# A weight cast copied ahead of time in DRAM, its loads on another queue, and an ACT step reordered, in an eight-core scan and feed-forward kernel

## The chip, the cores and the metric

The kernel runs on the 8 cores of one Trainium2 chip. Each core does the same program on its own quarter of the work: one of 4 batches, one half of the 2048 positions (1024 columns, and 64 columns of history ahead of them). The cores don't talk to each other. The metric is the device time in microseconds (us) of the slowest core. The kernel before takes 2141.85 us (median of 3 runs, 2139.96 to 2142.64).

A core has these engines: TensorE (PE, matrix products), VectorE (DVE), ScalarE (ACT), GpSimd (POOL) and SyncE (SP). DMAs are issued here by POOL and by SP. Whatever POOL issues goes to a queue that the profile calls q0, software_dynamic; whatever SP issues goes to q1, hardware_dynamic. Both are served by the same 16 DMA engines of the core. In this kernel only POOL issues DMAs that change the type of the numbers on the way (float32 or int8 in memory, bfloat16 in the on-chip buffer).

## The reference, cut to what matters

```
x = x + layernorm(attn(layernorm(x)))        # layer "attn", a linear scan over positions
x = x + layernorm(ffn(layernorm(x)))         # int8 weights, silu(gate) * up, down

attn(x):  x_proj = x @ proj_in_w.T + proj_in_b
          delta  = softplus(x_proj @ B_w.T)
          h      = h * sigmoid(A) + x_proj_t * delta_t          (scan)
          y      = h.sum(states) @ C_w.T + D_param * x_proj
          return  (y @ proj_out_w.T + proj_out_b) + x
ffn(x):   down( silu((x @ w_gate) * s_gate) * ((x @ w_up) * s_up) ) * s_down
```

The sizes are 2048 channels, 8192 inner channels and 16 states. The change bears on `y @ proj_out_w.T` and on how its weight gets to the core.

## The kernel before, in words

Channels lie on the 128 partitions, in 16 tiles; the columns are positions. X, the input, stays in float32 in the on-chip memory (tile XT), loaded as three windows of columns: the last 64 columns by POOL, columns 0 to 511 (window 0 below) and 512 to 1023 (window 1) by SP. Every engine has one list of instructions, written in the order of the program and run in that order. `W(engine, tracker, value)` puts a wait on a counter into a list, `P` puts an instruction that counts up, `CB` makes an engine wait for its own last instruction, `DMA(queue, tracker, ...)` puts a transfer into a list, and `BAR` makes PE, DVE and ACT wait for each other. Nothing reorders the lists.

The stages, with their places in the profile of the kernel before:

- Constants. SP issues 13 small loads (L397), all counted on one tracker, and behind them the two large windows of X (L407). POOL issues its window of X, the small weight BWTT, and the first two of 16 tiles of the input weight (WRIT, L412).
- Pack (to 52 us). ACT waits for all 13 constants (the wait ahead of L421), then DVE and ACT build powers of sigmoid(A) in turns (L448, L461 on DVE, L457 on ACT).
- First layer norm (to 141 us). For each window, ACT makes a bfloat16 copy and a square of 16 tiles of XT (L485, L487), PE sums them over partitions, a short chain makes mean and scale, and DVE applies them (L573, L576), which writes XN1T. The order is: the 64 columns, window 0, window 1.
- Input projection (to 261 us): 16 output tiles, each with one weight tile WRIT of 128 x 2048, in two slots. POOL loads tile t+2 when PE is through tile t (L618).
- The scan, as products with packed powers (to 338 us), then `C_w` and `D_param` (to 393 us), which write YPRE: DVE writes the last of it at L739.
- Output projection (388 to 530 us), the stage that the change edits. 16 output tiles t; each has a weight tile WROT of 128 x 2048 in one of two slots and is done in two halves of 512 columns. POOL loads tiles 0 and 1 at L754 when PE is through the stage before, and tile t+2 at L822 when PE is through tile t. A half is 16 matmuls on PE; then ACT takes the sum out of PSUM and adds the bias (L779, into SQTT), DVE adds XN1T (L785), ACT squares the result (L792) and copies the half's columns of XT to bfloat16 (L797, into XBT, one buffer), and DVE multiplies that copy with the result (L803, into XYT). PE sums the three rows (result, square, product) over the partitions in `pend_sum`, which stands in PE's list behind the 16 matmuls of the next half; only after the last half does PE come to it at once. The tracker value that both the square's sum and DVE's product wait for is that of the second of the two ACT instructions, which is L797.
- Second layer norm (to 657 us), where the result is added to XT, and the feed-forward layer for the two windows in turn (to 2121 us), then the last store, issued by SP at L981.

Of the kernel before, what the change touches and what calls it, by code (L numbers as in the profile page):

```python
# [8 lines left out]
BF16 = mybir.dt.bfloat16  # L9
# [6 lines left out]
DT = 16  # L16
S = 16
TOUT = 1024
PAD = 64
# [49 lines left out]
def build_program(taps=()):  # L69
    nc = bass.Bass("TRN2", target_bir_lowering=False)  # L70

    d_x = nc.dram_tensor("xT", [128, DT * T], F32, kind="ExternalInput").ap()
    d_win = nc.dram_tensor("w_in_t", [DT, 128, 2048], F32, kind="ExternalInput").ap()
    d_wout = nc.dram_tensor("w_out_t", [DT, 128, 2048], F32, kind="ExternalInput").ap()
    d_bwt = nc.dram_tensor("b_w_t", [128, 256], F32, kind="ExternalInput").ap()
    d_cwt = nc.dram_tensor("c_w_t", [16, 2048], F32, kind="ExternalInput").ap()
    d_a = nc.dram_tensor("a_t", [128, 256], F32, kind="ExternalInput").ap()
# [17 lines left out]
    for tname, tshape, tdt in taps:  # L95
        tap_out[tname] = nc.dram_tensor("tap_" + tname, tshape, tdt,
                                        kind="ExternalOutput").ap()

    al = Alloc(SBUF_BYTES)
# [48 lines left out]
    o_xyt = al.pin(180224, 512 * 2, 4, 6, "xyt0")  # L148
    o_xyt2 = al.pin(209344, 512 * 2, 4, 6, "xyt1")
    o_xbt = al.pin(191232, 512 * 2, 4, 6, "xbt")  # L150
    o_invb0 = al.pin(206848, 512 * 2, 5, 7, "invb0")
    import os as _os
    if _os.environ.get("KDEBUG_ALLOC"):
# [6 lines left out]
    def Praw(eng, fn):  # L160
        plan[eng].append(fn)

    t_pe, t_vec, t_scl = Trk("t_pe"), Trk("t_vec"), Trk("t_scl")
# [4 lines left out]
    s_wro = [Trk(f"s_wro{i}", 16) for i in range(2)]  # L168
    s_wrf = [Trk(f"s_wrf{i}", 16) for i in range(4)]
    s_wrd = [Trk(f"s_wrd{i}", 16) for i in range(2)]  # L170
    s_out, s_tap = Trk("s_out", 16), Trk("s_tap", 16)
    DMAT = ([s_const] + s_x + [s_bwt, s_cwt] + s_wri + s_wro + s_wrf + s_wrd
            + [s_out, s_tap])
    TRKS = [t_pe, t_vec, t_scl] + DMAT
    ETRK = {"tensor": t_pe, "vector": t_vec, "scalar": t_scl}

    def DMA(queue, trk, build):
        trk.n += trk.step
        plan[queue].append(lambda e, b=build, t=trk: b(e).then_inc(t.h, t.step))
        return (trk, trk.n)  # L180

    def W(eng, trk, val=None):
        if val is None:
            trk, val = trk
        if val and val > 0:
            Praw(eng, lambda e, t=trk, v=val: e.wait_ge(t.h, v))

    def P(eng, fn):
        trk = ETRK[eng]
        trk.n += trk.step  # L190
        plan[eng].append(lambda e, b=fn, t=trk: b(e).then_inc(t.h, t.step))
        return trk.n
# [10 lines left out]
    def CB(eng):  # L203
        trk = ETRK[eng]
        Praw(eng, lambda e, t=trk, v=trk.n: e.wait_ge(t.h, v))
# [53 lines left out]
    def REG(name, off, part, cols, dtype):  # L259
        return nc.alloc_sbuf_tensor_at(name, [part, cols], dtype,  # L260
                                       offset=arena_base + off).ap()
# [29 lines left out]
    XYR0 = REG("XYR0", o_xyt, 1, 512, BF16)  # L291
    XYR1 = REG("XYR1", o_xyt2, 1, 512, BF16)
    XBT = REG("XBT", o_xbt, 128, 512, BF16)
    INVB0 = REG("INVB0", o_invb0, 128, 512, BF16)

    def SQT(i):
# [17 lines left out]
    def WRI(i):  # L314
        return WRIT[:, i * 2048:(i + 1) * 2048]
# [32 lines left out]
    def Xj(j, c0, c1):  # L348
        return XT[:, j * T + c0:j * T + c1]
# [7 lines left out]
    def YATT(j, l0, l1):  # L357
        return XPBT[:, j * T + l0:j * T + l1]
# [51 lines left out]
    for t in range(2):  # L410
        v_win[t] = DMA("gpsimd", s_wri[t % 2],
                       lambda e, t=t: e.dma_start(out=WRI(t % 2), in_=d_win[t]))  # L412

    P("vector", lambda e: e.memset(DLY, 0.0))
    v_dly = M("vector")
# [10 lines left out]
                                              in0=SCR[:, 0:256], scalar1=1.0))  # L426
# [6 lines left out]
                                       in1=SCR[:, 0:256]))  # L433
    CB("vector")
    P("vector", lambda e: e.tensor_mul(out=SIG8, in0=SCR[:, 256:512],
                                       in1=SCR[:, 256:512]))
# [10 lines left out]
    for o in range(1, NO):  # L447
        P("vector", lambda e, o=o: e.tensor_tensor(  # L448
            out=pkf4[:, :, o, :], in0=pkf4[:, :, o - 1, :], in1=siga3,
# [119 lines left out]
    def ln1_apply(wi, c0, c1, v_chain):  # L569
        wl = c1 - c0  # L570
        W("vector", t_scl, v_chain)
        for j in range(DT):
# [15 lines left out]
                                        in_=SRA1[0:1, PAD:PAD + 1024]))  # L588
    P("vector", lambda e: e.tensor_copy(out=XROWB[0:1, 0:1024],
                                        in_=SRB1[0:1, PAD:PAD + 1024]))  # L590
# [4 lines left out]
    for t in range(DT):  # L595
# [19 lines left out]
        if t + 2 < DT:  # L615
            W("gpsimd", t_pe, t_pe.n)
            v_win[t + 2] = DMA("gpsimd", s_wri[t % 2],
                               lambda e, t=t: e.dma_start(out=WRI(t % 2),  # L618
                                                          in_=d_win[t + 2]))
# [6 lines left out]
    for wi, (w0, w1) in enumerate(WIN3):  # L626
# [3 lines left out]
        for j in range(DT):  # L630
# [5 lines left out]
            out=SCR[0:16, 0:wl], in_=pb[b][0:16, 0:wl], func=AF.Exp))  # L636
        CB("scalar")
        P("scalar", lambda e, wl=wl: e.activation(
            out=SCR[0:16, 512:512 + wl], in_=SCR[0:16, 0:wl], func=AF.Ln,
# [3 lines left out]
            out=DB[:, w0:w1], in_=SCR[0:16, 512:512 + wl]))  # L643
# [6 lines left out]
    for wi, (w0, w1) in enumerate(WIN3):  # L650
# [7 lines left out]
            out=DR[:, w0:w1], in_=pb[b][:, 0:wl]))  # L658
# [8 lines left out]
    for k in range(2):  # L667
# [4 lines left out]
        for g in range(NG):  # L672
            for pi, (p0, p1) in enumerate(pieces):
# [3 lines left out]
                for j in range(DT):  # L677
# [6 lines left out]
                      out=GH(g, p0 - gb, p1 - gb), in0=pb[b][:, 0:pl],  # L684
                      in1=DR[:, p0:p1], op=ALU.mult))
# [3 lines left out]
            if g == 0:  # L689
                P("vector", lambda e: e.tensor_copy(  # L690
                    out=ACC1[:, 0:519], in_=GH(0, 57, 576)))
            else:
                c0 = 57 - 8 * g
                P("vector", lambda e, c0=c0, g=g: e.tensor_add(
                    out=ACC1[:, 0:519], in0=ACC1[:, 0:519],
                    in1=GH(g, c0, c0 + 519)))
# [10 lines left out]
        for o in range(NO):  # L707
# [5 lines left out]
            out=SHB[:, 512 * k:512 * (k + 1)], in_=pb[b][0:16, 0:512]))  # L713
# [10 lines left out]
    for t in range(DT):  # L724
        for wi in range(2):
            l0 = wi * 512
# [7 lines left out]
                out=SCR[:, 0:512], in_=XPBj(t, PAD + l0, PAD + l0 + 512),  # L734
# [5 lines left out]
                out=YPRE(t, l0, l0 + 512), in0=pb[b][:, 0:512],  # L740
                in1=SCR[:, 0:512]))
# [6 lines left out]
    BAR()  # L748
    WL2 = [(0, 512), (512, 1024)]
    v_wout = {}  # L750
    W("gpsimd", t_pe, t_pe.n)
    for t in range(2):
        v_wout[t] = DMA("gpsimd", s_wro[t % 2],
                        lambda e, t=t: e.dma_start(out=WRO(t % 2),  # L754
                                                   in_=d_wout[t]))
    W("tensor", t_vec, v_ypre)
    for b_ in (4, 5, 6, 7):
        pe_acquire(banks[b_])
    v_yatt_prev = {0: 0, 1: 0}
    sq_prev = {0: 0, 1: 0}  # L760
    xy_prev = {0: 0}
    xym_prev = {0: 0, 1: 0}
    pend_sum = None
    for t in range(DT):
        W("tensor", v_wout[t])
        for wi in range(2):
            l0 = wi * 512
            bk = banks[(t * 2 + wi) % 4]
            pe_acquire(bk)
            for j in range(DT):  # L770
                mm(pb[bk.idx][:, 0:512], WRO(t % 2)[:, j * 128:(j + 1) * 128],
                   YPRE(j, l0, l0 + 512), j == 0, j == DT - 1)
            bk.w_pe = t_pe.n
            if pend_sum is not None:
                pend_sum()
            sl = (t * 2 + wi) % 2
            W("scalar", t_pe, bk.w_pe)
            W("scalar", t_vec, v_yatt_prev[sl])
            P("scalar", lambda e, t=t, b=bk.idx, sl=sl: e.activation(  # L779
                out=SQT(sl)[:, 0:512], in_=pb[b][:, 0:512], func=AF.Identity,  # L780
                bias=BOUTC[:, t:t + 1]))
            vsc = M("scalar")
            bk.r_trk = (t_scl, vsc)
            W("vector", t_scl, vsc)
            P("vector", lambda e, t=t, l0=l0, sl=sl: e.tensor_add(  # L785
                out=YATT(t, l0, l0 + 512), in0=SQT(sl)[:, 0:512],
                in1=XN1j(t, PAD + l0, PAD + l0 + 512)))
            vv = M("vector")
            v_yatt_prev[sl] = vv
            W("scalar", t_vec, vv)  # L790
            W("scalar", t_pe, sq_prev[sl])
            P("scalar", lambda e, t=t, l0=l0, sl=sl: e.activation(  # L792
                out=SQT(2 + sl)[:, 0:512], in_=YATT(t, l0, l0 + 512),
                func=AF.Square))
            CB("scalar")
            W("scalar", t_vec, xy_prev[0])
            P("scalar", lambda e, t=t, l0=l0: e.copy(  # L797
                out=XBT, in_=Xj(t, PAD + l0, PAD + l0 + 512)))
            vsq = M("scalar")
            xyt_t = XYT0 if sl == 0 else XYT1  # L800
            W("vector", t_scl, vsq)
            W("vector", t_pe, xym_prev[sl])
            P("vector", lambda e, t=t, l0=l0, d=xyt_t: e.tensor_mul(  # L803
                out=d, in0=XBT, in1=YATT(t, l0, l0 + 512)))
            vxy = M("vector")
            xy_prev[0] = vxy

            def pend_sum(t=t, wi=wi, l0=l0, sl=sl, vv=vv, vsq=vsq, vxy=vxy,
                         xyt_t=xyt_t):
                W("tensor", t_vec, vv)  # L810
                mm(pb[6 if wi == 0 else 7][0:1, 0:512], ONESB,
                   YATT(t, l0, l0 + 512), t == 0, t == DT - 1)
                W("tensor", t_scl, vsq)
                sq_prev[sl] = mm(pb[4 if wi == 0 else 5][0:1, 0:512], ONESB,
                                 SQT(2 + sl)[:, 0:512], t == 0, t == DT - 1)
                W("tensor", t_vec, vxy)
                xym_prev[sl] = mm(pb[6 if wi == 0 else 7][32:33, 0:512],
                                  ONESB, xyt_t, t == 0, t == DT - 1)
        if t + 2 < DT:
            W("gpsimd", t_pe, t_pe.n)  # L820
            v_wout[t + 2] = DMA("gpsimd", s_wro[t % 2],
                                lambda e, t=t: e.dma_start(out=WRO(t % 2),  # L822
                                                           in_=d_wout[t + 2]))
    pend_sum()
    for b_ in (4, 5, 6, 7):
        banks[b_].w_pe = t_pe.n
# [173 lines left out]
    for k in range(2):  # L1000
        l0 = 512 * k
# [276 lines left out]
```

## Time and profile before

| | us |
|---|---|
| median of 3 runs | 2141.85 |
| the profiled execution's own time | 2140.66 |
| its span, first to last instruction, core 2 | 2139.0 |
| PE busy | 1754.3 (82%) |
| DVE busy | 415.2 (19%) |
| ACT busy | 335.1 (16%) |
| POOL busy | 155.3 (7%) |

The profile is of one execution on the slowest core. Its page gives for each engine the busy time and for 40 equal slices of the span the busy share in tenths; the granted PE clock and the share of the 16 DMA engines that is in use stand beside them. Two layers are to be told apart: the feed-forward layer fills the span from 657 us on, mostly with matmuls that follow each other closely, and the first 141 us hold only short sums. All eight cores have spans from 2134.7 to 2139.0 us.

### The profile page before, as it was taken

The numbers are of one execution on the slowest core, as the hardware profiler recorded it, in microseconds if no ns is written. First come the engines' busy times: TensorE is split into PE (matmuls) and PEld (weight loads), VectorE is DVE, ScalarE is ACT, GpSimd is POOL, SyncE is SP. The second block draws the span as 40 slices with busy tenths as digits, with TensorE's granted clock in tenths as the row PEclk, the third lists the DMA queues.
The fourth block names the chain that finished last, engine by engine and source line by source line (L and its number), as shares of the span: only waits on it lengthen the run. The fifth ranks groups of instructions, "written<-read, shape, count | busy, mean of one in ns | idle before, by whom it ended". The sixth has DMA issues, their size and how long they took to land.

```text
span 2139.0 us, 20851 instructions; the slowest of 8 cores (2134.7 to 2139.0 us)
## 1 busy us (share of the span) xinstructions
PE 1754.3 (82%) x8040; PEld 750.2 (35%) x8199; DVE 415.2 (19%) x705; ACT 335.1 (16%) x563; POOL 155.3 (7%) x295
## 2 busy tenths in 40 slices
PE   0659985698026999999999999799999999899980
PEld 0024441233013444444443333244444444333330
DVE  3440023222773111011100000311111011500005
ACT  3712202444010100110100000001101112000010
POOL 0000000000000000000001111000000000111100
PEclk9989997799568999999999999799999999999995
DMA  6014200233002443444333333234433443533322
GB/s 194 1 20 69 50 1 2 50 64 64 21 28 91 157 154 143 156 157 169 146 133 133 138 128 135 78 144 156 157 147 149 157 153 123 187 133 133 133 103 79
DMA packets 51509, 237.24 MB, mean 111 GB/s; under 512 B 5811, under 2 KB 6196, under 8 KB 35028
## 3 DMA queue, kind: packets, MB, share of 16 engines
q0 software_dynamic: 41792, 218.78, 30.8%
q1 hardware_dynamic: 9620, 17.11, 2.4%
q8 instruction: 68, 1.11, 0.2%
q14 instruction: 29, 0.24, 0.0%
HBM read 143.73 MB, written 8.39 MB: 71 GB/s over the span
## 4 chain that ended last, share of the span: by engine, by line
PE 71%; DVE 11%; DMA 9%; issue 3%; ACT 3%; DVEq 0%; SPq 0%; ACTq 0%; POOLq 0%
PE pb L225 71%; DMA WRDAT<-wd_t 4%; DMA WRDBT<-wd_t 4%; DVE SQT L573 1%; DVE XT L937 1%; DVE SCRT L934 1%; ACT SCRT L733 1%; DVE YPRE L739 1%; DVE SQTT L931 1%; DVE XN1T L576 1%; DVE PKF L461 1%; DVE SCRT L969 1%; DVE SQTT L942 1%; DVE XT L972 1%; DVE SQTT L1005 1%
## 5 line engine op out<-in xcount | busy, mean ns | idle before, releaser
L225 PE MATMUL pb<-X2NAT,WGUA 128*128 128x512 bf16 x2007 | 443.8, 381 | 92.7 <-DVE SCRT L898 70.5
L225 PE MATMUL pb<-X2NBT,WGUB 128*128 128x512 bf16 x2007 | 447.5, 382 | 17.3 <-DVE X2NBT L1009 14.3
L225 PEld LDWEIGHTS pb<-X2NAT,WGUA 128*128 128x128 bf16 x2048 | 201.2, 98 | 335.8 <-issue 97.1
L225 PEld LDWEIGHTS pb<-X2NBT,WGUB 128*128 128x128 bf16 x2048 | 200.8, 98 | 264.1 <-issue 26.2
L225 PE MATMUL pb<-FUSETB,WRDBT 128*128 128x512 bf16 x1002 | 232.3, 384 | 26.2 <-DMA WRDBT<-wd_t 24.1
L225 PE MATMUL pb<-FUSETA,WRDAT 128*128 128x512 bf16 x1003 | 227.9, 379 | 18.2 <-DMA WRDAT<-wd_t 14.6
L1047 ACT ACTIVATE SCRT<-pb,SGC 128x512 f32<-128x512 f32 x128 | 88.0, 687 | 831.8 <-PE pb L225 803.5
L225 PEld LDWEIGHTS pb<-FUSETB,WRDBT 128*128 128x128 bf16 x1024 | 97.1, 98 | 160.9 <-issue 56.9
L225 PEld LDWEIGHTS pb<-FUSETA,WRDAT 128*128 128x128 bf16 x1024 | 96.3, 97 | 149.7 <-issue 41.8
L225 PE MATMUL pb<-XN1T,WRIT 128*128 128x512 bf16 (+1 forms) x752 | 121.7, 322 | 23.2 <-DVE XN1T L576 21.1
L1054 DVE SCALAR_TENSOR_TENSOR FUSETB<-pb,SUC,SCRT 128x512 bf16<-128x512 f32 x64 | 48.1, 751 | 395.2 <-PE pb L225 395.2
L225 PE MATMUL pb<-YPRE,WROT 128*128 128x512 bf16 x500 | 116.2, 383 | 8.5 <-DMA WROT<-w_out_t 7.7
L1054 DVE SCALAR_TENSOR_TENSOR FUSETA<-pb,SUC,SCRT 128x512 bf16<-128x512 f32 x64 | 48.1, 751 | 384.1 <-PE pb L225 382.9
L225 PE MATMUL pb<-SQTT,ONESB 128*1 128x512 bf16 (+1 forms) x160 | 60.8, 440 | 72.3 <-ACT SQTT L485 55.1
L1141 DVE CAST SRNT<-pb 1x512 bf16<-1x512 f32 x2 | 1.4, 678 | 481.5 <-PE pb L225 481.5
L225 PEld LDWEIGHTS pb<-XN1T,WRIT 128*128 128x128 bf16 x768 | 58.7, 99 | 86.9 <-issue 29.0
L225 PEld LDWEIGHTS pb<-YPRE,WROT 128*128 128x128 bf16 x512 | 48.0, 99 | 75.4 <-issue 23.3
L1062 POOL DMA_DIRECT2D WGUA<-wgu_t x62 | 32.9, 530 | 509.9 <-PE pb L225 509.9
L1062 POOL DMA_DIRECT2D WGUB<-wgu_t x62 | 32.9, 530 | 418.1 <-PE pb L225 418.1
L225 PE MATMUL pb<-XPBT,PKT 128*128 128x64 bf16 (+1 forms) x378 | 49.1, 292 | 1.5 <-ACT DRT L657 1.1
L1112 POOL DMA_DIRECT2D WRDBT<-wd_t x62 | 32.9, 530 | 225.3 <-PE pb L225 225.3
L1112 POOL DMA_DIRECT2D WRDAT<-wd_t x62 | 32.9, 530 | 212.4 <-PE pb L225 212.4
(130 smaller groups left out, 737.5 us busy)
## 6 DMA issues: line engine op xcount, KB each, us to landing
WGUA<-wgu_t POOLq DMA_DIRECT2D x64, 1024.0 KB, 4.9
WGUB<-wgu_t POOLq DMA_DIRECT2D x64, 1024.0 KB, 4.9
WRDAT<-wd_t POOLq DMA_DIRECT2D x64, 512.0 KB, 3.4
WRDBT<-wd_t POOLq DMA_DIRECT2D x64, 512.0 KB, 3.4
WRIT<-w_in_t POOLq DMA_DIRECT2D x16, 512.0 KB, 6.1
XT<-xT SPq DMA_DIRECT2D x2, 4096.0 KB, 28.5
WROT<-w_out_t POOLq DMA_DIRECT2D x16, 512.0 KB, 5.2
out_xT<-XT SPq DMA_DIRECT2D x2, 4096.0 KB, 15.7
```

What stands on the lines that cost most here:

```text
L225: e.matmul(o, l, r, start=st, stop=sp))
L461: P("vector", lambda e: e.tensor_mul(out=PKF, in0=PKF, in1=S8R))
L573: P("vector", lambda e, j=j, c0=c0, c1=c1, wl=wl: e.tensor_sub(out=SQT4[:, 0:wl], in0=Xj(j, c0, c1), in1=MB1F[:, 0:wl]))
L576: P("vector", lambda e, j=j, c0=c0, c1=c1, wl=wl: e.tensor_mul(out=XN1j(j, c0, c1), in0=SQT4[:, 0:wl], in1=INV1B[:, 0:wl]))
L733: P("scalar", lambda e, t=t, l0=l0: e.activation(out=SCR[:, 0:512], in_=XPBj(t, PAD + l0, PAD + l0 + 512), func=AF.Copy, scale=DCOL[:, t:t ...
L739: P("vector", lambda e, t=t, l0=l0, b=bk.idx: e.tensor_add(out=YPRE(t, l0, l0 + 512), in0=pb[b][:, 0:512], in1=SCR[:, 0:512]))
L931: P("vector", lambda e, j=j, c0=c0, wl=wl, src=src: e.tensor_sub(out=SQT(3)[:, 0:wl], in0=src, in1=MB_B[:, 0:wl]))
L934: P("vector", lambda e, j=j, c0=c0, wl=wl: e.tensor_mul(out=CH2[:, 0:wl], in0=SQT(3)[:, 0:wl], in1=INVB[:, 0:wl]))
L1047: P("scalar", lambda e, i=i, b=bg.idx: e.activation(out=GS, in_=pb[b][:, 0:512], func=AF.Silu, scale=SGC[:, i:i + 1]))
L1054: P("vector", lambda e, i=i, k=k, b=bu.idx: e.scalar_tensor_tensor(out=FUSE(k, i), in0=pb[b][:, 0:512], scalar=SUC[:, i:i + 1], in1=GS, op ...
L1062: lambda e, i=i, k=k, s=slg(i): e.dma_start(out=WGUPW(k, s), in_=d_wgu[i + 2]))
L1112: lambda e, p=pre, k=k: e.dma_start(out=WRDW(k, p[1] % 2), in_=d_wd[p[0], p[1] // 2, :, (p[1] % 2) * 2048: (p[1] % 2 + 1) * 2048]))
```

## The change

A scratch tensor `wout_bf` in DRAM is added, in bfloat16. At the start of the program POOL issues 16 DMAs that copy the output weight from its float32 input tensor to it, DRAM to DRAM, with the change of type, behind the first two WRIT tiles. SP waits for all 16 and for PE, and then loads the WROT tiles from `wout_bf`; it also issues tiles 2 to 15. In the half of the output projection, ACT's copy of XT goes ahead of the square and no longer behind it, with a second buffer XBT2 (so that DVE's product of the half before isn't waited for) and one more wait of ACT for itself.

```diff
+    d_woutb = nc.dram_tensor("wout_bf", [DT, 128, 2048], BF16, kind="Internal").ap()
+    o_xbt2 = al.pin(210368, 512 * 2, 4, 6, "xbt2")
+    s_wpc = Trk("s_wpc", 16)
+    XBT2 = REG("XBT2", o_xbt2, 128, 512, BF16)
...
     for t in range(2):
         v_win[t] = DMA("gpsimd", s_wri[t % 2],
                        lambda e, t=t: e.dma_start(out=WRI(t % 2), in_=d_win[t]))
+    v_wpre = {}
+    for t in range(DT):
+        v_wpre[t] = DMA("gpsimd", s_wpc,
+                        lambda e, t=t: e.dma_start(out=d_woutb[t],
+                                                   in_=d_wout[t]))
...
-    W("gpsimd", t_pe, t_pe.n)
+    W("sync", t_pe, t_pe.n)
+    W("sync", v_wpre[DT - 1])
     for t in range(2):
-        v_wout[t] = DMA("gpsimd", s_wro[t % 2],
+        v_wout[t] = DMA("sync", s_wro[t % 2],
                         lambda e, t=t: e.dma_start(out=WRO(t % 2),
-                                                   in_=d_wout[t]))
+                                                   in_=d_woutb[t]))
...
-    xy_prev = {0: 0}
+    xy_prev = {0: 0, 1: 0}
...
             vv = M("vector")
             v_yatt_prev[sl] = vv
+            xbt_t = XBT if sl == 0 else XBT2
+            CB("scalar")
+            W("scalar", t_vec, xy_prev[sl])
+            P("scalar", lambda e, t=t, l0=l0, d=xbt_t: e.copy(
+                out=d, in_=Xj(t, PAD + l0, PAD + l0 + 512)))
+            CB("scalar")
             W("scalar", t_vec, vv)
             W("scalar", t_pe, sq_prev[sl])
             P("scalar", lambda e, t=t, l0=l0, sl=sl: e.activation(
                 out=SQT(2 + sl)[:, 0:512], in_=YATT(t, l0, l0 + 512),
                 func=AF.Square))
-            CB("scalar")
-            W("scalar", t_vec, xy_prev[0])
-            P("scalar", lambda e, t=t, l0=l0: e.copy(
-                out=XBT, in_=Xj(t, PAD + l0, PAD + l0 + 512)))
             vsq = M("scalar")
...
-            P("vector", lambda e, t=t, l0=l0, d=xyt_t: e.tensor_mul(
-                out=d, in0=XBT, in1=YATT(t, l0, l0 + 512)))
+            P("vector", lambda e, t=t, l0=l0, d=xyt_t, s=xbt_t: e.tensor_mul(
+                out=d, in0=s, in1=YATT(t, l0, l0 + 512)))
             vxy = M("vector")
-            xy_prev[0] = vxy
+            xy_prev[sl] = vxy
...
         if t + 2 < DT:
-            W("gpsimd", t_pe, t_pe.n)
-            v_wout[t + 2] = DMA("gpsimd", s_wro[t % 2],
+            W("sync", t_pe, t_pe.n)
+            v_wout[t + 2] = DMA("sync", s_wro[t % 2],
                                 lambda e, t=t: e.dma_start(out=WRO(t % 2),
-                                                           in_=d_wout[t + 2]))
+                                                           in_=d_woutb[t + 2]))
```

POOL's list at the start of the program and up to the feed-forward weights, before (the shape is rows x elements of one DMA's destination, `x16` a count):

```order
L407 DMA XT<-xT 128x16x64
L408 DMA BWTT<-b_w_t 128x256
L412 DMA WRIT<-w_in_t 128x2048 x2
L618 DMA WRIT<-w_in_t 128x2048 x14
L703 DMA CWTT<-c_w_t 16x2048
L754 DMA WROT<-w_out_t 128x2048 x2
L822 DMA WROT<-w_out_t 128x2048 x14
L831 DMA WGUA<-wgu_t 128x4096 x2
```

The same place of POOL's list, after:

```order
L411 DMA XT<-xT 128x16x64
L412 DMA BWTT<-b_w_t 128x256
L416 DMA WRIT<-w_in_t 128x2048 x2
L420 DMA wout_bf<-w_out_t 16x16384 x16
L627 DMA WRIT<-w_in_t 128x2048 x14
L712 DMA CWTT<-c_w_t 16x2048
L843 DMA WGUA<-wgu_t 128x4096 x2
```

The 16 WROT loads have left POOL's list, and 16 DMAs to `wout_bf` stand behind the first two WRIT loads. Both sides of such a copy lie in one piece in DRAM, and the built program takes it as 16 rows of 16384 elements, where a WRIT or WROT load has 128 rows of 2048.

SP's list from the last constant, before:

```order
L397 DMA IDENTF<-ident_f 128x128
L407 DMA XT<-xT 128x16x512 x2
L981 DMA out_xT<-XT 2048x1x512 x2
```

And after:

```order
L401 DMA IDENTF<-ident_f 128x128
L411 DMA XT<-xT 128x16x512 x2
L764 DMA WROT<-wout_bf 128x2048 x2
L834 DMA WROT<-wout_bf 128x2048 x14
L993 DMA out_xT<-XT 2048x1x512 x2
```

The WROT loads stand between the loads of X and the first store; nothing that SP had to issue stands between the first of them and the last.

ACT's list at the first two halves of the output projection, before:

```order
L779 ACTIVATE SQTT<-pb,BOUTC 128x512
L792 ACTIVATE SQTT<-XPBT 128x512
L797 CAST XBT<-XT 128x512
L779 ACTIVATE SQTT<-pb,BOUTC 128x512
L792 ACTIVATE SQTT<-XPBT 128x512
L797 CAST XBT<-XT 128x512
```

And after, where `XBT_64` is the second buffer:

```order
L789 ACTIVATE SQTT<-pb,BOUTC 128x512
L803 CAST XBT<-XT 128x512
L808 ACTIVATE SQTT<-XPBT 128x512
L789 ACTIVATE SQTT<-pb,BOUTC 128x512
L803 CAST XBT_64<-XT 128x512
L808 ACTIVATE SQTT<-XPBT 128x512
```

The copy has gone ahead of the square, so it stands where ACT waited for DVE's addition; it is the same in all 32 halves.

## Rows read from the trace of the kernel before

**Rows 1.** The page: PE's busy time, its and the DMAs' slices.
```profile
PE 1754.3 (82%) x8040; PEld 750.2 (35%) x8199; DVE 415.2 (19%) x705; ACT 335.1 (16%) x563; POOL 155.3 (7%) x295
...
PE   0659985698026999999999999799999999899980
...
DMA  6014200233002443444333333234433443533322
```

**Rows 2.** The chain that ended last, in time: start us, length us, what.
```profile
7.54 10.23 DMA IDENTF<-ident_f
...
28.18 1.91 ACT PKT L457
30.17 2.30 DVE PKF L461
```

**Rows 3.** Timeline, start to PE's first full product: start, length, engine, line, operation, names, wait.
```profile
17.85 0.42 ACT L421 ACTIVATE SCRT<-SIGA 128x256 f32<-128x256 f32 x1 [10.62 <-DMA IDENTF<-ident_f]
...
62.94 0.61 ACT L485 CAST SQTT<-XT 128x512 bf16<-128x512 f32 x1
...
90.79 0.61 ACT L485 CAST SQTT<-XT 128x512 bf16<-128x512 f32 x1
...
141.33 6.74 PE L225 MATMUL pb<-XN1T,WRIT 128*128 128x512 bf16 x34 [21.10 <-DVE XN1T L576]
```

**Rows 4.** Tensor xT: issues (ns each, first and last start us), time to landing.
```profile
L407 SPq DMA_DIRECT2D XT<-xT x2: 684/5611/10538, 7.9 to 8.7; - x2
...
DMA to landing us min/median/max: 8.3/22.3/34.7
```

**Rows 5.** DMA queues, 0 to 14 us: packets, MB, share of 16 engines.
```profile
q0 software_dynamic: 528, 1.50, 66.3%
q1 hardware_dynamic: 1066, 0.27, 10.1%
```

**Rows 6.** DMA queues, 10 to 14 us.
```profile
q0 software_dynamic: 171, 0.63, 95.9%
q1 hardware_dynamic: 187, 0.07, 9.4%
```

**Rows 7.** DMA queues, 0 to 18 us.
```profile
q0 software_dynamic: 576, 1.64, 56.7%
q1 hardware_dynamic: 1727, 1.08, 23.7%
```

**Rows 8.** DMA queue, 18 to 42 us.
```profile
q1 hardware_dynamic: 3721, 7.57, 94.5%
```

**Rows 9.** DMA queue, 406 to 410.5 us, one WROT load.
```profile
q0 software_dynamic: 144, 0.52, 69.7%
```

**Rows 10.** The page: all DMA packets by size, and those of q1.
```profile
DMA packets 51509, 237.24 MB, mean 111 GB/s; under 512 B 5811, under 2 KB 6196, under 8 KB 35028
...
q1 hardware_dynamic: 9620, 17.11, 2.4%
```

**Rows 11.** Timeline, start of the output projection.
```profile
388.05 1.09 POOL L754 DMA_DIRECT2D WROT<-w_out_t  x2 [53.54 <-PE pb L225]
...
392.52 0.69 DVE L739 TENSOR_TENSOR YPRE<-pb,SCRT 128x512 bf16<-128x512 f32 x1 [0.92 <-ACT SCRT L733]
394.82 0.14 PEld L225 LDWEIGHTS pb<-YPRE,WROT 128*128 128x128 bf16 x2 [7.83 <-issue]
395.23 8.45 PE L225 MATMUL pb<-YPRE,WROT 128*128 128x512 bf16 x31 [7.74 <-DMA WROT<-w_out_t]
```

**Rows 12.** Busy time, 400 to 526 us: us, engines' busy us, PEclk, DMA share, GB/s.
```profile
400.00:526.00 126.00, 125.11 (x577) 48.53 (x585) 26.38 (x62) 59.97 (x93) 7.42 (x14) 1.00 0.35 59
```

**Rows 13.** Timeline, the last half of the output projection.
```profile
526.30 0.69 ACT L779 ACTIVATE SQTT<-pb,BOUTC 128x512 bf16<-128x512 f32 x1 [1.33 <-PE pb L225]
527.09 0.42 DVE L785 TENSOR_TENSOR XPBT<-SQTT,XN1T 128x512 bf16<-128x512 bf16 x1 [1.52 <-ACT SQTT L779]
...
527.95 0.63 ACT L792 ACTIVATE SQTT<-XPBT 128x512 bf16<-128x512 bf16 x1 [0.95 <-DVE XPBT L785]
528.72 0.62 ACT L797 CAST XBT<-XT 128x512 bf16<-128x512 f32 x1
...
529.51 0.43 DVE L803 TENSOR_TENSOR XYT<-XBT,XPBT 128x512 bf16<-128x512 bf16 x1 [1.99 <-ACT XBT L797]
```

**Rows 14.** DMA issues of the whole run, stores of the result.
```profile
out_xT<-XT SPq DMA_DIRECT2D x2, 4096.0 KB, 15.7
```

More of the change, by code:

```diff
@@ L171, in build_program @@
     s_out, s_tap = Trk("s_out", 16), Trk("s_tap", 16)
+    s_wpc = Trk("s_wpc", 16)
     DMAT = ([s_const] + s_x + [s_bwt, s_cwt] + s_wri + s_wro + s_wrf + s_wrd
-            + [s_out, s_tap])
+            + [s_out, s_tap, s_wpc])
     TRKS = [t_pe, t_vec, t_scl] + DMAT
```

## The prediction

> **What bounds the kernel now.** I read the page's slices first: PE is busy 82% of the span, and the stretches where it isn't are the first three slices, the layer norms and the last slice, while the DMA engines reach their full share nowhere but near the start [rows 1]. The chain that ended last tells what the start hangs on: a DMA of the last constant, 10.23 us long, and behind it DVE and ACT taking turns at the pack [rows 2]. So I read the first 141 us in the timeline, and the two DMA queues in short windows there; then the two ends of the output projection.
>
> In the timeline ACT starts its first real work at 17.85 us, after 10.62 us of waiting for the constants; it starts on window 0 of X at 62.94 us and on window 1 at 90.79 us, and PE starts the input projection at 141.33 us [rows 3]. Everything from 17.85 us to there is one chain on ACT, DVE and (for sums) PE, so whatever delays the constants moves the whole program by as much. The windows of X have slack: SP issues window 0 at 7.9 and window 1 at 8.7 us, they land 22.3 and 34.7 us later (8.3 is POOL's small window), at 30 and 43 us [rows 4], 33 and 47 us ahead of their need. Matmuls, waits and clocks after 141 us don't depend on it.
>
> In the output projection PE is busy 125.11 of 126 us at the full granted clock (2.4 GHz) while ACT is busy 59.97 and the DMA engines 35% [rows 12]. PE is the bound there. Only the ends of the stage are open: the start waits for WROT, the end for the chain ACT, DVE, ACT, DVE.
>
> **Loads of WROT by SP in bfloat16.** Before, POOL issues at 388.05, the weights are read on PE from 394.82 and the first matmul is at 395.23; YPRE is ready at 392.52 + 0.69 = 393.21 [rows 11]. A tile takes 0.697 x 4.5 = 3.14 us of all 16 DMA engines [rows 9]. From bfloat16 the same 0.52 MB at the rate of the loads of X, 7.57 MB in 24 us or 0.315 MB per us [rows 8], take 1.7 us. What lies around a transfer on SP's queue I take from the stores: 15.7 us for 4.19 MB, of which 13.3 is transfer at that rate, leaves 2.4 us [rows 14]. That lands at 388.1 + 4.1 = 392.2, ahead of YPRE. PE can't start before 393.4, so the gain is 394.82 - 393.4 = 1.4 us, and no faster load makes it more. Below: if SP's path took 6.7 us, 0. Value 1.4. Tiles 2 to 15 are hidden before and after: a tile of matmuls lasts 8.2 us there (126 us for 15.4 tiles), and a load is shorter. SP has nothing else to issue in the stage; behind its waits stands only the store of the end. POOL loses 16 issues that nobody waited for.
>
> **ACT's order.** In 31 of 32 halves PE has the next 16 matmuls before it needs the rows, and it is busy over 99% of the stretch, so nothing is won or lost; the added wait of ACT for itself, about 0.1 us, has 66 us of idle ACT time over it. After the last half the path is L779 at 526.30, DVE's addition to 527.51, the square at 527.95, the copy at 528.72, and DVE's product at 529.51 [rows 13]. After the change the copy runs from 527.07 to 527.69 beside the addition, the square from about 527.8 to 528.45, and the product starts at about 528.6. Gain 0.9 us; bounds 0.6 (the copy alone) and 1.1.
>
> **The 16 copies in DRAM.** This is the term that decides. They stand in q0 right behind the two WRIT loads, so they start on each DMA engine when its WRIT rows are done. What shares the engines with them is q1: the constants and then the windows of X.
>
> How the engines divide themselves shows between 10 and 14 us, when both queues have work: q0 gets 171 packets and q1 187, which is one for one, but q0's packets are the 4 KB rows of WRIT and take 95.9% of the time, and q1's, mostly short rows of constants, 9.4% [rows 6]. A packet there is a row: the 3721 packets of 18 to 42 us carry 2034 B each, the 2 KB rows of X [rows 8]. So a long row in q0 makes a short row in q1 wait for its whole length. That is why the last constant takes 10 us to land.
>
> The Trainium skill (DMA: Bandwidth & Descriptors, Queues, rings and completion order) says that each DMA engine goes round its queues at packet granularity and switches at packet boundaries only. The trace agrees, 171 to 187.
>
> How many constants are left when the copies start: the 13 constant loads have 1186 rows, and a closing packet for each engine that takes part, 178, so 1364 packets (the page's 9620 packets of q1 are these, the 8192 rows of X in and out, and 64 closing ones [rows 10]). At 14 us 1066 of them are through [rows 5], 298 are left, 19 an engine. Of q0's 576 packets [rows 7] 528 are through [rows 5], 48 are left, 3 an engine. Going one for one, 19 - 3, say 15, constant packets an engine are still waiting when the copies begin, at about 15.2 us (14 + 3 x 0.4). Before, they then drain at once, and ACT goes on at 17.85.
>
> How long one row of a copy is: each has 16384 elements, a sixteenth of a tile, so an engine has one row of each of the 16 tiles, and a row takes as long as a tile does on 16 engines. Lower end: 3.14 us, the WROT load of the same data with the same cast [rows 9]. Upper end: the tile's bytes in memory, 1.05 MB read and 0.52 MB written, all at the 0.315 MB per us that eight cores got together while loading X [rows 8], 5.0 us. I take 3.7, a third of the way, since the WROT load is the nearest row.
>
> The Trainium skill (HBM Reference, Specifications (TRN2)) gives about 358 GB/s as a core's share of the memory. No run here shows a copy in DRAM; by that figure a row would be an estimated 4.4 us, and the delay below 66 us.
>
> So the constants land 15 x 3.7 = 55.5 us later (15 x 3.14 = 47 to 15 x 5.0 = 75; all 16 rows are the cap, 50 to 80). The copies end at 15.2 + 16 x 3.7 = 74 us. Then window 0 of X, 4.2 MB, needs 13.3 us and lands near 90, where ACT now needs it at 62.94 + 55.5 = 118; window 1 lands at 103, needed at 146. WRIT tile 2, issued by POOL after PE's first tile, finds q0 empty. So the copies cost what they cost the constants and nothing more.
>
> **Sum.** 55.5 - 1.4 - 0.9 = +53.2 us. Against the profiled execution's 2140.66 (span 2139.0 and 1.7 around it) that is 2193.9. The median of the runs is 1.2 above that execution: 2195 us, slower by 2.5%. This case's own range is 47 - 2.3 to 75 - 2.3, or 2187 to 2215.
>
> **Rivals.**
>
> *The turn is a piece, not the row.* If the engine cuts the 64 KB rows into pieces like a WRIT row (8 KB read, 4 KB written), each piece is 0.39 us, and an engine has 128 of them. The 15 constants are then late by 15 x 0.39 = 6 us. But window 0 of X has 128 rows an engine of 0.1 us (22.7 us over 233 rows [rows 8]) against 113 pieces that are left: 21 + 113 x 0.49 = 76 us, the last 15 rows and 2 us of landing make 80, where it is needed at 69. Together 17 us late, less 2.3: 2157. With pieces of 0.62 us (the 5.0 us tile) it is 21 to 24 + 113 x 0.72 + 3.5 = 109, needed at 72, so 46 late: up to 2186. For it: nothing in q0 before is as long as 64 KB. Against: the page counts 51509 - 35028 = 16481 packets of 8 KB and more, which are the 16384 rows of the 128 loads of WGUA and WGUB [rows 10]; rows of that size at least aren't cut.
>
> The Trainium skill (DMA: Bandwidth & Descriptors, SWDGE vs HWDGE vs iDMA) wants packets of at most 4096 B, "preferably". Cut so, the pieces would be of this rival's size; the 8 KB packets of this trace speak against it.
>
> *Not slower: the engines share by time.* If a long row doesn't hold its engine, because rows of both queues are in flight at once and bytes decide, q1 gets half the time. The constants' 15 rows are short and cost under 1 us. Window 0 gets 0.16 MB per us from 15.2 us: 4.2 MB land at 44, before 62.94; window 1 at 70, before 90.79. The copies are covered by slack, and the two gains are left: 2141.85 - 2.3 = 2139.6, up to 2141 with 1 us for the constants. For it: the slack of 33 and 47 us. Against: the 95.9% to 9.4% between 10 and 14 us, while q1 had a backlog. It decides from the place where fewer than one or two constant rows an engine are left behind the WRIT rows, which 19 against 3 at 14 us contradicts.
>
> *More than the constants and the gains.* If the memory gives less than 0.315 MB per us to reads and writes together, the rows are longer than 5 us and the time is over 2215; or the start of the stage gains more than I see, which YPRE bars: for over 0.2% faster 4.3 us are needed, and the parts have 2.5 at most.
>
> **How the numbers follow.** Rows as turns 0.52, pieces 0.19, shared by time 0.21, longer than 2215 us 0.05, faster for a reason I don't see 0.03. The prediction is that of the first case. The range 2139 to 2214 takes in the first three cases but for their tails, and leaves out the last two and about a third of the shared case. A measurement of this kernel can tell about 0.2% (4.3 us) from no change; of the cases, the pieces and the rows are slower than that, the shared case is the same: faster 0.03, same 0.21, slower 0.76.
>
> **What the new profile would show.** Right: ACT's L421 (the first activation that reads SIGA) starts at 65 to 90 us behind a wait for a constant; q1 has about one packet for each packet of q0 while both have work, and hardly any bytes; q0 is empty at 65 to 95 us; the pack and the layer norm follow unchanged in length; PE's first full product comes as much later as L421 does; the wait for WROT ends 1.4 us sooner against YPRE; the last half of the stage is 0.9 us shorter. Wrong: L421 near 18 us. If then ACT waits for XT at window 0, it is the pieces; if it doesn't, the sharing. If L421 is late but by much less than q0 lasts, my count of rows left is wrong.

## The result and the profile after

The changed kernel takes 2186.92 us (median of 10 runs) against 2142.6 us for the kernel before on the same chips: a ratio of 1.0209, 95% interval 1.0198 to 1.0220. That is 44 to 45 us slower; the forecast was 2195 us, 53 slower, in a range from 2139 to 2214. In some executions of every kernel a few cores, or one half of the chip, had a lower granted clock than the rest and were longer, so the ratios have wide intervals, and the table of the experiments gives beside them the median span of the cores in the profiled execution (for e1, e10 and e11 of the four cores of the half that had none of these). The profiled execution took 2187.05 us, its span on the slowest core (5) is 2185.0, which is 46.0 more than the span before.

The page of the changed kernel shows the DMA engines' slices. Of the 40 slices of 54.6 us the first two are full, the third and fourth are busy for 10 to 20%.

```profile
PE 1761.1 (81%) x8199; PEld 751.1 (34%) x8199; DVE 415.2 (19%) x705; ACT 334.7 (15%) x563; POOL 153.9 (7%) x295
...
DMA  9911410011101444444433443144444433544332
```

The timeline of the changed kernel answers to [rows 3]: ACT's first work on SIGA, its start on windows 0 and 1 of X, and PE's first run of the input projection after the layer norm.

```profile
8.18 86.92 SPq L411 DMA_DIRECT2D XT<-xT  x2
63.73 0.42 ACT L430 ACTIVATE SCRT<-SIGA 128x256 f32<-128x256 f32 x1 [56.50 <-DMA IDENTF<-ident_f]
...
108.83 0.61 ACT L494 CAST SQTT<-XT 128x512 bf16<-128x512 f32 x1
...
135.30 0.61 ACT L494 CAST SQTT<-XT 128x512 bf16<-128x512 f32 x1
...
185.85 6.34 PE L228 MATMUL pb<-XN1T,WRIT 128*128 128x512 bf16 x33 [21.29 <-DVE XN1T L585]
```

L430 is late by 63.73 - 17.85 = 45.9 us, window 0 by 45.9, window 1 by 44.5 and PE by 44.5. The whole loss is there before ACT does its first work. On the eight cores L430 starts between 60.9 and 63.7 us, where it was 15.9 to 18.0 before. The rest of the program is moved: the first product on XYR, behind the output projection, comes 42.9 us later (579.2 against 536.3), the two gains of that stage off, and from there to the end it is 1605.8 us against 1602.7. These are different cores; core 2, the slowest before, takes 1603.8 after.

The DMA queues of the changed kernel between 18 and 30 us and between 18 and 60 us (packets, MB, share of 16 engines) answer to [rows 6]; the first line is all packets of the shorter stretch by size.

```profile
DMA packets 176, 1.44 MB, mean 120 GB/s; under 512 B 132, under 2 KB 132, under 8 KB 132
...
q0 software_dynamic: 88, 1.44, 108.0%
q1 hardware_dynamic: 88, 0.00, 0.7%
...
q0 software_dynamic: 280, 4.59, 98.2%
q1 hardware_dynamic: 280, 0.13, 2.2%
```

Packet for packet they are even, 88 to 88 and 280 to 280, and q1 has 2.2% of the time. The 1.44 MB of q0 are 44 rows of 32 KB (as written); the other 44 of its 88 packets are under 512 B: one for each row, which I read as the short packet with which a DMA closes on every engine. As q1 has 88 packets to all 88 of q0, the closing packet is a turn of its own. A tile's copy takes 0.524 MB / (4.59 MB / 42 us) = 4.8 us.

How the constants get through shows in q1's packets up to 15.2 us, when the copies begin, and up to 54 us.

```profile
q1 hardware_dynamic: 1099, 0.27, 10.5%
...
q1 hardware_dynamic: 1361, 0.34, 4.0%
```

Of the constants' 1364 packets 265 are left at 15.2 us, 16.6 for each engine on average. At two turns for each 4.8 us these need 40 us, to 55 us, and at 54 us all but a few are through. ACT goes on at 63.73: the last few constants, which come about 9 us after the others, decide. The view doesn't show the engines one by one; that these few belong to an engine with more constants than the others is my reading.

The tensors xT and w_out_t in the changed kernel: issues, and time from issue to landing (us, min/median/max), of X and of the copies. They answer to [rows 4].

```profile
L411 SPq DMA_DIRECT2D XT<-xT x2: 774/43436/86099, 8.2 to 9.0; - x2
...
DMA to landing us min/median/max: 7.4/97.0/109.7
...
L420 POOL DMA_DIRECT2D wout_bf<-w_out_t x16: 522/550/588, 4.5 to 11.7; - x16
...
DMA to landing us min/median/max: 16.0/48.4/81.5
```

The last copy lands at 11.7 + 81.5 = 93 us. Window 0 of X lands at 8.2 + 97.0 = 105.2, which is 3.6 us ahead of the 108.83 at which ACT takes it. That is core 5; on cores 4 and 6 of the same execution ACT waited 0.6 us for it.

The output projection of the changed kernel, the time from issue to landing of its 16 loads of WROT, its start (answers to [rows 11]), its middle (to [rows 12]) and its last half (to [rows 13]):

```profile
DMA to landing us min/median/max: 3.1/3.2/4.3
...
431.59 0.83 SPq L764 DMA_DIRECT2D WROT<-wout_bf  x2
436.47 0.69 DVE L748 TENSOR_TENSOR YPRE<-pb,SCRT 128x512 bf16<-128x512 f32 x1 [0.92 <-ACT SCRT L742]
438.15 4.43 PE L228 MATMUL pb<-YPRE,WROT 128*128 128x512 bf16 x10 [6.70 <-DVE YPRE L748]
...
443.00:569.00 126.00, 126.00 (x588) 48.67 (x587) 26.39 (x62) 59.97 (x93) 0.00 (x0) 1.00 0.18 59
...
570.02 0.69 ACT L789 ACTIVATE SQTT<-pb,BOUTC 128x512 bf16<-128x512 f32 x1 [1.80 <-PE pb L228]
570.81 0.42 DVE L795 TENSOR_TENSOR XPBT<-SQTT,XN1T 128x512 bf16<-128x512 bf16 x1 [2.00 <-ACT SQTT L789]
570.85 0.62 ACT L803 CAST XBT<-XT 128x512 bf16<-128x512 f32 x1
...
571.67 0.63 ACT L808 ACTIVATE SQTT<-XPBT 128x512 bf16<-128x512 bf16 x1 [0.20 <-ACT XBT L803]
...
572.47 0.42 DVE L815 TENSOR_TENSOR XYT<-XBT,XPBT 128x512 bf16<-128x512 bf16 x1 [1.24 <-ACT SQTT L808]
```

PE now waits for YPRE and no longer for the weights; from YPRE's end to the first matmul it is 438.15 - 437.16 = 1.0 us, where it was 395.23 - 393.21 = 2.0. ACT's copy lies beside DVE's addition, and from L789 to the product L815 it is 2.45 us, where it was 3.21. Both gains are there, 1.0 and 0.8 us, and both are small.

### The profile page after: what moved, and what is told of

It is laid out like the page before. It is cut to its first block, busy times and chain, and to the rows that moved or that the text cites. A ratio compares the mean times of both kernels' runs of the same rounds, so it can differ in the third digit from the quotient of the medians.

```text
span 2185.0 us, 21058 instructions; the slowest of 8 cores (2177.8 to 2185.0 us)
## 1 busy us (share of the span) xinstructions
PE 1761.1 (81%) x8199; PEld 751.1 (34%) x8199; DVE 415.2 (19%) x705; ACT 334.7 (15%) x563; POOL 153.9 (7%) x295
## 4 chain that ended last, share of the span: by engine, by line
PE 68%; DVE 11%; DMA 10%; ACT 4%; issue 3%; another core or an unknown queue 3%; DVEq 0%; ACTq 0%; POOLq 0%
PE pb L228 68%; DMA WRDBT<-wd_t 5%; DMA WRDAT<-wd_t 4%; ACT SCRT L742 1%; DVE SQT L582 1%; DVE XT L949 1%; DVE SCRT L946 1%; DVE YPRE L748 1%; DVE SQTT L943 1%; DVE XN1T L585 1%; DVE PKF L470 1%; DVE SCRT L981 1%; DVE SQTT L954 1%; DVE XT L984 1%
## 5 line engine op out<-in xcount | busy, mean ns | idle before, releaser
L228 PEld LDWEIGHTS pb<-SQTT,ONESB 128*1 128x1 bf16 x160 | 10.7, 81 | 146.9 <-issue 146.9
```

Source lines behind the costliest of these rows:

```text
L228: e.matmul(o, l, r, start=st, stop=sp))
```

## The experiments

Ratios are against runs of the kernel before on the same chip. The median span is that of the profiled execution, as said with the result; the last column is of its slowest core.

| | median span of the cores | ratio, 95% interval | ACT's work on SIGA |
|---|---|---|---|
| before | 2137.7 | | 17.85 |
| after | 2180.4 | 1.0209 (1.0198 to 1.0220) | 63.73 |
| e1, 16 copies | 2181.6 | 1.0278 (1.0249 to 1.0308) | 60.17 |
| e2, 12 copies | 2184.0 | 1.017 (1.0088 to 1.0251) | 62.92 |
| e3, 6 copies | 2165.5 | 1.0122 (1.007 to 1.0174) | 46.13 |
| e4, short rows | 2180.5 | 1.0236 (1.0147 to 1.0325) | 24.51 |
| e5, late copies | 2135.8 | 1.0012 (0.9992 to 1.0032) | 17.01 |
| e6, after + SIGA | 2177.6 | 1.0228 (1.014 to 1.0316) | 7.37 |
| e7, before + SIGA | 2126.7 | 0.9948 (0.9903 to 0.9993) | 7.37 |
| e8, late + SIGA | 2127.4 | 0.9973 (0.9932 to 1.0015) | 7.38 |
| e9, ACT's order | 2136.8 | 0.998 (0.9943 to 1.0017) | 17.67 |
| e10, SIGA + order | 2126.9 | 0.9944 (0.9903 to 0.9984) | 7.38 |
| e11, e8 again | 2128.7 | 0.9968 (0.9933 to 1.0002) | 7.38 |

**e1, the copies alone.** To the kernel before, only this is added (and a wait of POOL for them at the very end):

```diff
+    for t in range(16):
+        v_wpre = DMA("gpsimd", s_wpc,
+                     lambda e, t=t: e.dma_start(out=d_woutb[t], in_=d_wout[t]))
```

> The kernel before with only the 16 copies added at the start (nothing reads them; WROT is loaded as before, ACT's order as before). Theory (turns: the constants behind the copies cost everything): ACT's first work on SIGA at 63 to 65 us instead of 17.85, so +46, and none of the two gains of the output projection: 2188 to 2190 us. Rival (part of the 44 us comes from the loads of WROT by SP or from ACT's order): under 2180 us.

ACT went on at 60.2 us on this core, 3 us sooner than expected, and between 61.3 and 64.3 on the other seven. Cores 4 to 7 have a median span 45 us above theirs before (2181.6 against 2136.6). The ratio is higher than expected for the reason given with the result. The copies alone make the loss.

**e2 and e3, fewer copies.** The edit is `range(12)` and `range(6)` in e1.

> The kernel before with only the first 12 of the 16 copies added at the start, nothing reads them. Theory (19 constant packets an engine, two turns of a copy for each tile of 4.8 us, so that the constants are through after 9 to 10 tiles): the last 4 tiles don't matter to the constants, ACT's first work stays at 63 to 65 us: 2186 to 2190 us, as with 16. Rival (the constants wait for the copies' bytes in proportion, or for their end): three quarters, ACT's first work at 52 us, 2177 us.

> The kernel before with only the first 6 of the 16 copies added at the start, nothing reads them. Theory: 12 turns of an engine, less than its 19 constant packets, so the constants land when the copies are through, at about 15 + 6 x 4.8 = 44 us, with 2 us of landing ACT starts at 45 to 47 us, 28 us late: 2169 to 2172 us. Rival (proportion of the bytes, 6 of 16 of 46 us): 17 us late, 2160 us.

ACT's first work on SIGA in e2, then in e3 (timelines):

```profile
62.92 0.42 ACT L426 ACTIVATE SCRT<-SIGA 128x256 f32<-128x256 f32 x1 [55.69 <-DMA IDENTF<-ident_f]
```

```profile
46.13 0.42 ACT L426 ACTIVATE SCRT<-SIGA 128x256 f32<-128x256 f32 x1 [38.90 <-DMA IDENTF<-ident_f]
```

Four copies fewer change nothing, ten fewer give 14 to 18 us back. A loss in proportion to the bytes would have been at 52 and 35 us. So a count decides. In the changed kernel the last constant is through after about (63.7 - 15.2) / 4.8 = 10 tiles: fewer than 12, so the last tiles don't matter, and more than 6, so with 6 tiles the constants are through when the copies are, 15.2 + 6 x 4.8 + 2 of landing = 46.0.

**e4, short rows.** The same copies, with a gap behind each row of the scratch tensor, so that a copy is 128 rows of 2048 numbers, 8 on each engine:

```diff
-    d_woutb = nc.dram_tensor("wout_bf", [DT, 128, 2048], BF16, kind="Internal").ap()
+    d_woutb = nc.dram_tensor("wout_bf", [DT, 128, 2112], BF16, kind="Internal").ap()
...
-                        lambda e, t=t: e.dma_start(out=d_woutb[t],
+                        lambda e, t=t: e.dma_start(out=d_woutb[t, :, 0:2048],
```

> The changed kernel, but each tile of the scratch tensor has rows of 2112 numbers, of which 2048 are used, so that a copy has 128 rows of 2048 numbers where it had 16 of 16384. Theory (one row of the constants' queue passes for each packet of the copies, whatever its length): a tile of 4.8 us now is 9 turns of an engine of 0.53 us, so the 19 constant packets of an engine wait 10 us and ACT starts at about 28 us; window 0 of X then has its 128 rows an engine against the rest of the 144 turns, and lands at about 105 to 110 us, needed at 73: the program is late by 42 to 47, with ACT's wait now ahead of window 0. 2182 to 2190 us. Rival (what counts is how many bytes the copies move, both queues share them in time): ACT starts at 63 us as with the long rows. Second rival (short rows are fair to X as well): 2145 to 2160 us.

ACT's two late starts in e4 (timeline), then the two queues in e4 from 24 to 60 us:

```profile
24.51 0.42 ACT L430 ACTIVATE SCRT<-SIGA 128x256 f32<-128x256 f32 x1 [17.29 <-DMA IDENTF<-ident_f]
...
106.96 0.62 ACT L494 CAST SQTT<-XT 128x512 bf16<-128x512 f32 x1 [37.28 <-DMA XT<-xT]
```

```profile
q0 software_dynamic: 920, 3.34, 69.3%
q1 hardware_dynamic: 921, 1.89, 28.9%
```

The constants come 39 us sooner than with long rows, at 24.5 us (3.5 sooner than I expected; on the other cores 25.4 to 27.8), and the program is as slow as before this edit, because ACT now waits 37.28 us for window 0 of X. 920 packets to 921: it is turns again. Window 0 of X lands at nearly the same time in the changed kernel, in e4 and in e6 below (105, 107 and 106 us), since it waits for the copies whatever their rows are.

**e5, the copies behind X.**

```diff
+    W("gpsimd", v_xw[0])
+    W("gpsimd", v_xw[1])
     for t in range(DT):
         v_wpre[t] = DMA("gpsimd", s_wpc,
```

> The changed kernel, but POOL waits for both large windows of X to land before it issues the 16 copies. Theory: the constants and X land as in the kernel before, the copies run from 43 to about 120 us beside ACT, DVE and PE, which they don't touch, and end ahead of WRIT tile 2 at 148 us: ACT starts at 17.9 us, and only the gains of the output projection are left, 1 us at its start and 0.8 at its end: 2140 to 2142 us. Rival (the copies' traffic or POOL's work slows the layer norm or DVE too): over 2150 us.

In e5 the first of these lines shows ACT's start; the second is the busy times of the layer norm, 63 to 110 us, and the third is q0 from 30 to 130 us. The last line is the same stretch of 63 to 110 us in the kernel before.

```profile
17.01 0.42 ACT L432 ACTIVATE SCRT<-SIGA 128x256 f32<-128x256 f32 x1 [9.78 <-DMA IDENTF<-ident_f]
...
63.00:110.00 47.00, 33.01 (x66) 3.85 (x66) 26.05 (x65) 37.25 (x68) 0.00 (x0) 1.00 1.01 112
...
q0 software_dynamic: 512, 8.39, 75.1%
```

```profile
63.00:110.00 47.00, 32.38 (x64) 3.72 (x64) 25.87 (x66) 38.03 (x70) 0.00 (x0) 1.00 0.00 1
```

All 8.39 MB are copied with the DMA engines full, and ACT, DVE and PE do their layer norm beside it as before: busy for 33.0, 26.1 and 37.3 us (PE, DVE, ACT) where it was 32.4, 25.9 and 38.0. The spans are 1.9 us shorter than before, as expected; the ratio, 1.0012 with 1 inside its interval, can't tell it from no change. The copies cost what they make others wait for, and nothing that these runs show for their traffic.

**e6 and e7, the first constant on its own tracker.** In e6 on the changed kernel, in e7 on the kernel before:

```diff
+    v_siga = DMA("sync", s_siga, lambda e: e.dma_start(out=SIGA, in_=d_a))
-    for (dst, src) in [(SIGA, d_a), (DCOL, d_dcol), (BINC, d_bin),
+    for (dst, src) in [(DCOL, d_dcol), (BINC, d_bin),
...
-    W("vector", v_consts)
-    W("scalar", v_consts)
+    W("vector", v_siga)
+    W("scalar", v_siga)
...
     v_pack_vec = t_vec.n
+    for eng in ("vector", "scalar", "tensor"):
+        W(eng, v_consts)
```

> The changed kernel, but the first constant, SIGA, has a tracker of its own, and the pack waits for that one alone; the other 12 are waited for ahead of the first layer norm. Theory (X is a second wait right behind that of the constants): the pack is done by 42 us, the other constants land at 64, but window 0 of X still lands at 105 us, where the kernel before needed it at 63, so only 3 to 4 us are won back: 2182 to 2184 us. Rival (the constants alone cost the 46 us, X has slack, as I predicted): ACT goes on at 64 us with what it did at 52 before, about 2152 us.

> The kernel before, with a tracker of its own for SIGA, the pack waiting for that one alone. Theory (the wait for the other 12 constants is on the path of the whole program, one us for one us): the pack starts at about 8 us, when ACT is through its table copies, so 10 us sooner; the layer norm starts at 42, X has landed by then at 30 and 43 us: 2131 to 2133 us. Rival (the start is covered by something later): within 0.2% of 2142 us.

ACT's starts in e6 (timeline):

```profile
7.37 0.42 ACT L432 ACTIVATE SCRT<-SIGA 128x256 f32<-128x256 f32 x1
...
61.34 0.24 ACT L498 CAST SQTT<-XT 128x64 bf16<-128x64 f32 x1 [19.85 <-DMA IDENTF<-ident_f]
...
106.50 0.62 ACT L498 CAST SQTT<-XT 128x512 bf16<-128x512 f32 x1 [34.31 <-DMA XT<-xT]
```

In e6 the pack starts 56 us sooner, and the spans are 2.8 us shorter than after, no more: ACT then waits 20 us for the constants and 34 for window 0. In e7, where nothing is in X's way, the same edit is worth 17.85 - 7.37 = 10.5 us of wait and 11 us of span (2126.7 against 2137.7). So the wait for the constants is on the path for its full length only as long as X has landed behind it.

**e8 to e11, what is left when the copies are out of the way.** e8 and e11 are e5 and e6 together; e9 is the kernel before with ACT's new order alone; e10 is e7 and e9 together, with no copies at all.

> The changed kernel with both: POOL waits for both large windows of X before the copies, and SIGA has a tracker of its own. Theory: the 10 us of the pack and the 2 us of the output projection add up: 2129 to 2132 us, ahead of both kernels. Rival: the copies now lie beside the layer norm for longer and cost some of it back, over 2135 us.

> The kernel before with ACT's new order and the second buffer alone; no copies, WROT loaded by POOL as before. Theory: in 31 of 32 halves nothing, after the last half 0.8 us less between the last matmul on YPRE and the first sum of XYR (10.5 us before); the time within 0.2% of before. Rival (the extra wait of ACT for itself costs in each half): PE no longer busy over 99% of the stage, 3 us or more slower.

> The kernel before with a tracker of its own for SIGA and ACT's new order; no copies in DRAM. Theory: 10.5 us at the start and 0.8 in the output projection: 2129 to 2131 us, ratio 0.995, ahead of both kernels. Rival (ACT's order or the early pack gives it back later): ratio over 0.998.

> The changed kernel with the copies behind both windows of X and a tracker of its own for SIGA, timed again in five rounds, beside the version without copies. Theory: the copies are worth only the up to 1 us that WROT is late at the start of the output projection: 2128 to 2131 us, no difference to the version without copies that a timing shows. Rival (25 MB of traffic in each core beside the layer norm cost something): 3 us or more slower than that version.

The last half in e9, and its busy times from 400 to 526 us:

```profile
525.00 0.69 ACT L781 ACTIVATE SQTT<-pb,BOUTC 128x512 bf16<-128x512 f32 x1 [1.80 <-PE pb L226]
...
527.44 0.43 DVE L807 TENSOR_TENSOR XYT<-XBT,XPBT 128x512 bf16<-128x512 bf16 x1 [1.23 <-ACT SQTT L800]
...
400.00:526.00 126.00, 124.48 (x574) 48.06 (x582) 26.41 (x63) 59.94 (x94) 7.38 (x14) 1.00 0.35 59
```

2.44 us from L781 to the product, as in the changed kernel: the order is worth 0.8 us at the end of the stage. PE is busy 124.48 of 126 us, where [rows 12] has 125.11. That isn't a cost of the order: the stage ends 1.3 us sooner on this core, so that more of this window lies behind it, and from 398 to 524 us PE is busy 125.12 of 126. A timing doesn't show these 0.8 us. e10 is faster than before, 0.9944 with an interval to 0.9984, and the median of its cores 0 to 3 is 2126.9 us; so it beats both kernels, and nearly all of that is the one tracker (e7: 2126.7); its fastest run took 2130.34 us. e8 and e11, with the copies and SP's loads, have 2127.4 and 2128.7: no better than e10. Their ratios have 1 inside the interval, so the 10 us that the expectation of e8 names stand in the spans and not in a timing. That the copies are worth nothing beside e10 is what the medians say; their intervals overlap, and 1 us either way stays open.

## Why the prediction was right, and where it was not

- **What decides: right.** The copies stand in the constants' way, packet for packet. The 171 to 187 of [rows 6] became 280 to 280. e1, e2, e3 and e4 each show it from another side. The time alone wouldn't tell: 2186.9 us is the lowest that this case allowed (2187 to 2215), and slow pieces reached up to 2186. The late L430 and the packets tell them apart.
- **How long a row is: too short.** I took 3.7 us, a third of the way from 3.14 to 5.0; it was 4.8. The upper bound was the good one: a copy moves 1.57 MB in memory in 4.8 us, 0.328 MB per us. e4, with other rows, moves 3 x 3.34 + 1.89 = 11.9 MB in 36 us, 0.331, and X alone had 0.315 [rows 8]. The nearest row, the load of WROT, had no write to memory in it. The Trainium skill's share of 358 GB/s (HBM Reference, Specifications (TRN2)) gave 4.4, nearer than my value; the measured 4.8 is above it.
- **How many rows the constants wait for: too many.** I counted 15 packets an engine behind 15 rows. The packets were about right on average, 16.6 at 15.2 us; the rows weren't. A copy has two turns, its row and its closing packet; I counted closing packets for the constants and not for the copies. That alone makes it 16.6 / 2 x 4.8 = 40 us. The second miss is the average: ACT waits for the last constant, and that one came about 9 us after nearly all others, which makes the measured 45.9, or 9.6 rows. The prediction's own sign was there: ACT's start is late by much less than q0 lasts, 63.7 us against 93, and for that it said that the count of rows left is wrong.
- **The sum: luck in part.** 3.7 x 15 = 55.5 stands in place of 4.8 x 9.6 = 45.9. The rows were too short and too many, and the two errors went against each other; with the right length and my count it would have been 72. The forecast was nearer than its terms.
- **X has slack: right for the wrong size.** I had window 0 landing near 90 us and needed at 118. It landed at 105.2 and was needed at 108.8. A wait hidden 3.6 us behind the first one, and on two cores not hidden at all, isn't slack to build on, as e6 shows.
- **Start of the output projection: 1.0 us for 1.4.** SP's loads landed before YPRE was ready at 437.16, by 432.0 + 4.3 = 436.3 at the latest (4.3 us behind the issue, where I had 4.1). But from YPRE to the first matmul PE needs 1.0 us, where I had allowed 0.6.
- **ACT's order: 0.8 for 0.9,** and nothing in the other 31 halves, as said.
- **The rivals.** The pieces did not happen: the rows of 64 KB read went as one packet, 44 of them in the 1.44 MB. e4 makes the pieces by hand and shows what was forecast for them, constants late by 7 us (6 forecast) and then X, late by 44 (46 for the slow pieces). Sharing by time did not happen either: q1 had 2.2% of the time and not half.

## What to carry to other kernels

Before moving a bulk transfer into an idle stretch, look at what else is in flight on the DMA engines there, on the other queue too, and count it in packets: each short packet waits for one long one, and whoever waits for all of them waits for the last, which came here 9 us behind nearly all others. A transfer that nobody needs for 400 us belongs behind the ones that somebody needs in 10, with a wait that says so (e5). And a common tracker for 13 loads makes the first user wait for the last one: one tracker more gave 11 us (e7), which the whole change was not able to.

## What the runs showed of the hardware

- The closing packet of a DMA is a turn of its own between queues (88 packets for 44 rows in 1.44 MB, and 88 of the other queue beside them).
- One row of 16384 numbers, 64 KB read and 32 KB written, held an engine for 4.8 us in one piece as far as the other queue was concerned.
- Copies in DRAM with a cast went at 0.33 MB per us of reads and writes together, eight cores at once. Whether the memory or the DMA engines, which the profile shows as 98% busy, set that rate wasn't told apart.
- SP was 87 us in the issue of its two loads of X (the row of 8.18 us above; 11.3 before), 86.1 of them in the second; whatever is next in its list would have waited as long. That its queue was full meanwhile is the likely reason and isn't shown.
